# Two-expert routing after attention: the experts' up products as three fp32r products, with weight parts made for each tile

## The reference, cut to what matters

```python
x = L0_attn_x                                   # (2, 1024, 512) float32: 2048 tokens
xn = _layernorm(x)
x = x + attention(xn) + ffn(xn)

def ffn(x):                                     # 8 experts, two for each token, I = 352
    probs = softmax(einsum('th,eh->te', x, gate_w))
    topw, sel = top_k(probs, 2)
    topw = topw / sum(topw)
    combine = zeros((T, E)).at[arange(T)[:, None], sel].add(topw)
    g, u = split(einsum('th,eoh->eto', x, w1))  # w1: (8, 704, 512), the up products
    act = silu(g) * u
    expert_out = einsum('eti,ehi->eth', act, w2)
    return einsum('eth,te->th', expert_out, combine)
```

## Time and profile before

| | |
|---|---|
| median of 3 executions | 932.34 us (927.40 to 936.08) |
| the profiled execution: time, span | 932.23 us, 930.4 us |
| busy: PE, PEld, DVE | 850.4, 524.0, 368.2 us |
| busy: ACT, POOL | 290.8, 272.6 us |
| granted TensorE clock, mean | 0.957 |
| `gu` matmuls of the tiles, L883 | x624, 197.4 us |
| `down` matmuls, L901 | x234, 107.0 us |

### The profile page before, as it was taken

The page is one execution under the profiler, slowest core; times in us unless marked ns, Lnnn a source line. Parts: engine busy times, 40 slices in busy tenths (PEclk is TensorE's granted clock), DMA queues, the critical chain, the costliest instruction groups (busy, mean ns, idle before and its releaser), DMA issues. The chain is left out here.

```text
span 930.4 us, 12421 instructions
## 1 busy us (share of the span) xinstructions
PE 850.4 (91%) x3661; PEld 524.0 (56%) x3662; DVE 368.2 (40%) x1137; ACT 290.8 (31%) x622; POOL 272.6 (29%) x352
## 2 busy tenths in 40 slices
PE   3889999389999999999999989999999999999990
PEld 3668988255555555555555434566666656666650
DVE  5983452574666666666674021111111111111110
ACT  3221221004545555556555400112221211222210
POOL 4781000305233242332331610033332323333330
PEclk9899999758999999999999998999999999999995
DMA  9386596876357666576730137536445455433326
GB/s 318 143 264 206 197 314 203 252 171 228 97 156 186 187 191 153 178 199 173 189 83 14 42 112 258 169 69 156 107 107 158 73 156 147 81 68 64 57 29 201
DMA packets 76716, 143.20 MB, mean 154 GB/s; under 512 B 12928, under 2 KB 26752, under 8 KB 76608
## 3 DMA queue, kind: packets, MB, share of 16 engines
q1 hardware_dynamic: 38192, 65.68, 22.7%
q10 hardware_dynamic: 29056, 58.28, 22.1%
q0 software_dynamic: 9424, 18.69, 10.8%
HBM read 81.21 MB, written 61.15 MB: 153 GB/s over the span
## 5 line engine op out<-in xcount | busy, mean ns | idle before, releaser
L1286 ACT ACTIVATE probs<-scores_t 128x512 f32<-128x512 f32 (+3 forms) x384 | 163.7, 492 | 143.8 <-PE scores_t L1413 130.2
L883 PE MATMUL gu<-w,rows_t 128*128 x624 | 197.4, 459 | 1.1 <-DVE o_t L849 1.1
L1390 PE MATMUL maxima<-k_stack,q_stack 96*128 96x512 f32 (+3 forms) x384 | 141.2, 388 | 14.7 <-DMA q_stack<-qk_hi 8.7
L883 PEld LDWEIGHTS gu<-w,rows_t 128*128 128x128 f32 x624 | 115.2, 190 | 69.7 <-issue 19.7
L1433 PE MATMUL o_acc<-probs,v_ones 128*64 128x512 f32 (+3 forms) x768 | 147.9, 507 | 0.0
L1413 PE MATMUL scores_t<-q_stack,k_stack 98*128 98x512 f32 (+3 forms) x384 | 138.0, 385 | 5.6 <-DMA q_stack<-row_lo 3.5
L1316 DVE CUSTOM_DVE_ANT_0 masked_scores<-maxima,mask_m 128x128 f32<-128x128 f32 (+3 forms) x256 | 121.3, 485 | 23.5 <-PE maxima L1390 19.3
L1320 DVE TENSOR_REDUCE mx<-maxima 128x1 f32<-128x512 f32 x128 | 88.2, 689 | 86.4 <-PE maxima L1390 86.3
L1413 PEld LDWEIGHTS scores_t<-q_stack,k_stack 98*128 98x128 f32 x384 | 73.1, 193 | 67.9 <-issue 42.2
L901 PE MATMUL down<-w,hidden_t 128*128 (+1 forms) x234 | 107.0, 592 | 0.8 <-DVE hidden_t L857 0.8
L1390 PEld LDWEIGHTS maxima<-k_stack,q_stack 96*128 96x128 f32 x384 | 76.8, 202 | 35.6 <-DVE mx L1320 9.9
(11 more groups left out here) (148 smaller groups left out, 930.7 us busy)
## 6 DMA issues: line engine op xcount, KB each, us to landing
w<-in_w_t SPq DMA_DIRECT2D x8, 1408.0 KB, 6.5
routed<-blank_row ACTq DMA_DIRECT2D x20, 514.0 KB, 6.9
rows<-routed ACTq DMA_DIRECT2D x39, 256.0 KB
qk_hi<-st_hi SPq DMA_DIRECT2D x32, 256.0 KB, 4.8
qk_lo<-st_lo SPq DMA_DIRECT2D x32, 256.0 KB, 6.1
q_stack<-qk_hi ACTq DMA_DIRECT2D x32, 256.0 KB, 4.1
k_stack<-qk_hi ACTq DMA_DIRECT2D x26, 256.0 KB, 5.2
v_all<-o_t SPq DMA_DIRECT2D x4, 1536.0 KB, 5.7
```

What stands on the lines that cost most here:

```text
L883: last = nc.tensor.matmul(gu[r][j][:, 0:I], rows_t[r][:, k * P:(k + 1) * P], w1[:, bass.ds(e, 1), k, j * I:(j + 1) * I].rearrange("p o n - ...
L1286: nc.scalar.activation(probs[:, k % PR, h, 0:w], scores_t[e % RING][:, 0:w], ACT.Exp).then_inc(exp_done, 1)
L1390: nc.tensor.matmul(mb[at % RING][:, 0:w], q_st[i][0:3 * HD, h, t * P:(t + 1) * P], k_st[i][0:3 * HD, h, c * CH:c * CH + w], start=True, st ...
```

## The change

The up products become three fp32r products each (24 matmuls for a tile in place of 8 fp32 ones, which the trace shows as 16 records). The rows are split in PSUM-to-SBUF copies: ScalarE makes `rows_hi`, VectorE `rows_lo`. The high and low parts of the expert's `w1` (128 x 4 x 704) are made anew for every tile, one tile ahead: four ScalarE copies and four VectorE subtractions, two of each ahead of the old work of the tile and two behind it. ScalarE and VectorE read the ring slot from memory into a register; PE tells ScalarE by `tile_ready` that the expert of the next tile has been loaded. Each expert gets at least one tile, by one more small VectorE operation in the router (the tile counts with these inputs stay as the router finds them, and the loops always run over 39).

```diff
+        link(V.tensor_scalar(tiles[:], tiles[:], 1.0, None, ALU.max))
...
-        rows_t = [m.sbuf(f"rows_t{r}", [P, D], F32) for r in range(2)]
+        rows_hi = [m.sbuf(f"rows_hi{r}", [P, D], F32R) for r in range(2)]
+        rows_lo = [m.sbuf(f"rows_lo{r}", [P, D], F32R) for r in range(2)]
+        w1_hi = [m.sbuf(f"w1_hi{r}", [P, DK, 2 * I], F32R) for r in range(2)]
+        w1_lo = [m.sbuf(f"w1_lo{r}", [P, DK, 2 * I], F32R) for r in range(2)]
...
@@ sync: weights
                 load_weights(e)
-            for e in range(RING_E):
-                announce(e)
+                if e:
+                    announce(e - 1)
+            announce(RING_E - 1)
@@ scalar
-                nc.scalar.copy(rows_t[r][:], turn_ps[:]).then_inc(turned_read, 1)
+                nc.scalar.copy(rows_hi[r][:], turn_ps[:]).then_inc(rows_hi_done, 1)
+            def up_weights_high(r, slot, ks):
+                for k in ks:
+                    nc.scalar.copy(w1_hi[r][:, k, :], w1_rows(slot, k)).then_inc(w1_hi_done, 1)
+            def await_up_weights(i):
+                if past(i, 2):
+                    act.wait_ge(gu_full, (i - 1) * 2)
+                act.wait_ge(tile_ready, i + 1)
+                return slot_at(act, i)
             def tile(i, r, half):
                 if past(i, 2):
                     y_to_sbuf(i - 2, r, half - 1)
+                if more:
+                    slot = await_up_weights(i + 1)
+                    up_weights_high(1 - r, slot, range(0, DK // 2))
                 act.wait_ge(gu_full, i * 2 + 1)
                 ...
                 nc.scalar.activation(gated[:], gu[r][0][:, 0:I], ACT.Silu).then_inc(silu_done, 1)
+                if more:
                     rows_to_sbuf(i + 1, 1 - r)
+                    up_weights_high(1 - r, slot, range(DK // 2, DK))
                 load_rows(i + 3, 1 - r)
             for a in range(LATE):
                 if a == LATE - 1:
+                    up_weights_high(0, await_up_weights(0), range(DK))
                     rows_to_sbuf(0, 0)
@@ vector
+            def rows_low(i, r):
+                dve.wait_ge(rows_hi_done, i + 1)
+                ...
+                nc.vector.tensor_tensor(rows_lo[r][:], turn_ps[:], as_f32(rows_hi[r][:]), ALU.subtract).then_inc(turned_read, 1)
+            def up_weights_low(i, r, slot, ks):
+                if past(i, 2):
+                    dve.wait_ge(gu_full, (i - 1) * 2)
+                for k in ks:
+                    dve.wait_ge(w1_hi_done, i * DK + (k + 1))
+                    nc.vector.tensor_tensor(w1_lo[r][:, k, :], w1_rows(slot, k), as_f32(w1_hi[r][:, k, :]), ALU.subtract).then_inc(w1_done, 1)
             def tile(i, r, half):
+                if more:
+                    slot = slot_at(dve, i + 1)
+                    up_weights_low(i + 1, 1 - r, slot, range(0, DK // 2))
                 hidden_to_sbuf(i - 1, 1 - r)
+                if more:
+                    rows_low(i + 1, 1 - r)
+                    up_weights_low(i + 1, 1 - r, slot, range(DK // 2, DK))
                 ...
                 nc.vector.tensor_tensor(hidden[r][:], gu[r][1][:, 0:I], gated[:], ALU.mult).then_inc(hidden_done, 1)
             for a in range(LATE):
                 ...                                   # the adds into o_t, L849
+                if a == LATE - 2:
+                    up_weights_low(0, 0, slot_at(dve, 0), range(DK))
+            rows_low(0, 0)
@@ tensor
+                    nc.tensor.matmul(out, hi, w1_hi[r][:, k, cols], start=(k == 0), stop=False)
+                    nc.tensor.matmul(out, hi, w1_lo[r][:, k, cols], start=False, stop=False)
+                    last = nc.tensor.matmul(out, lo, w1_hi[r][:, k, cols], start=False, stop=(k == DK - 1))
             def tile(i, r, half):
                 if past(i, 2):
+                    down_product(i - 2, r, slot_at(pe, i - 2))
+                announce_tile(i + 1)
                 pe.wait_ge(turned_read, i + 1)
                 ...
-                pe.wait_ge(expert_ready, e + 1)
+                pe.wait_ge(w1_done, i * DK + DK)
+            def announce_tile(i):
+                pe.wait_ge(expert_ready, expert_at(pe, i) + 1)
+                pe.sem_inc(tile_ready, 1)
```

More of the change, by code:

```diff
@@ L727, in run_tiles, with expert_at, slot_at, w1_rows @@
                 tile(i, i % 2, i // 2)
+        def expert_at(engine, i):
+            return engine.value_load(tile_expert[0:1, bass.ds(i, 1)], min_val=0, max_val=E - 1)
+        def slot_at(engine, i):
+            return engine.value_load(keep["tile_slot"][0:1, bass.ds(i, 1)], min_val=0, max_val=RING_E - 1)
+        def w1_rows(slot, k):
+            return w1[:, bass.ds(slot, 1), k, :].rearrange("p o n -> p (o n)")
         def past(i, least):
@@ L817, in tile @@
                     y_to_sbuf(i - 2, r, half - 1)
+                more = not (isinstance(i, int) and i == SLOT_TILES - 1)
+                if more:
+                    slot = await_up_weights(i + 1)
+                    up_weights_high(1 - r, slot, range(0, DK // 2))
                 act.wait_ge(gu_full, i * 2 + 1)
@@ L844, in _ @@
         def _(dve):
[L845 to L850, removed]
             def hidden_to_sbuf(i, r):
@@ L866, in tile @@
                 nc.vector.tensor_tensor(hidden[r][:], gu[r][1][:, 0:I], gated[:], ALU.mult).then_inc(hidden_done, 1)
+            for a in range(LATE):
+                at = EARLY + a
+                dve.wait_ge(proj_full, a + 1)
+                nc.vector.tensor_tensor(o_t[:, :, at * P:(at + 1) * P], gu[a % 2][a // 2 % 2][:].rearrange("p (g t) -> p g t", t=P),
+                                        res[:, at, :].rearrange("p (g t) -> p g t", t=P), ALU.add).then_inc(res_done, 1)
+                if a == LATE - 2:
+                    up_weights_low(0, 0, slot_at(dve, 0), range(DK))
+            rows_low(0, 0)
             run_tiles(dve, tile)
@@ L879, in turn_rows, with up @@
                 last.then_inc(turned, 1)
-            def up(i, r, e, j):
+            def up(i, r, j):
+                out = gu[r][j][:, 0:I]
                 for k in range(DK):
-                    last = nc.tensor.matmul(gu[r][j][:, 0:I], rows_t[r][:, k * P:(k + 1) * P],
-                                            w1[:, bass.ds(e, 1), k, j * I:(j + 1) * I].rearrange("p o n -> p (o n)"),
-                                            start=(k == 0), stop=(k == DK - 1))
+                    hi, lo = (t[r][:, k * P:(k + 1) * P] for t in (rows_hi, rows_lo))
+                    cols = slice(j * I, (j + 1) * I)
+                    nc.tensor.matmul(out, hi, w1_hi[r][:, k, cols], start=(k == 0), stop=False)
+                    nc.tensor.matmul(out, hi, w1_lo[r][:, k, cols], start=False, stop=False)
+                    last = nc.tensor.matmul(out, lo, w1_hi[r][:, k, cols], start=False, stop=(k == DK - 1))
                 last.then_inc(gu_full, 1)
@@ L904, in down_product @@
                 last.then_inc(y_full, 1)
[L906 to L910, removed]
             def tile(i, r, half):
                 if past(i, 2):
[L914 to L917, removed]
+                    down_product(i - 2, r, slot_at(pe, i - 2))
+                if not (isinstance(i, int) and i == SLOT_TILES - 1):
+                    announce_tile(i + 1)
                 pe.wait_ge(turned_read, i + 1)
@@ L935, in _ @@
                     pe.wait_ge(res_done, a - 3)
+                if a == LATE - 2:
+                    announce_tile(0)
                 if a == LATE - 1:
```

14 lines of the change are left out of this document (9 added, 5 removed).

## The result

The changed kernel takes 939.55 us (median of 20 executions, 934.18 to 945.84) against 932.34 for the kernel before: ratio 1.008, 95% interval 1.0057 to 1.0103. It is 0.8% slower: clear of the scatter between executions, and inside the 1% that the prediction called no change. (One of the 20 executions of the kernel before took 1116.68 us; it stands alone and isn't compared.) The profiled execution took 937.0 us, its span 935.1.

The account below looks back on a forecast made before the run. PE's instructions were taken to bound each tile, all else hidden. Saving 33.5 us, plus 4.6 start, 16 late tags and 11.5 clock, gives -1.4 from 932.2, so 930.8; forecast 930 us, range 908 to 955.

Parts of the forecast that it names:

- the sign: Whole kernel: slightly faster, the sum of terms being -1.4 us against the kernel before.
- the turning point: Tiles, under the port conflict rival: a ring over 7.5 us decides the sign, 37 tiles then giving back 10 us.
- What PE saves: Up products on PE: 0.86 us saved a tile, 8.08 to 7.22 us; 33.5 us over 39 tiles.
- What ACT and DVE get: Weight and row splits: ACT comes to 4.5 and DVE to 5.0 of 7.22 us a tile, covered as sums.
- The room: Chain from y to hidden_t before the down product: 0.55 us to spare, so PE still sets an undisturbed tile.
- The late tags: At the loads of experts 3 to 7, late y delays the down product 3.2 us, five times: +16 us.
- The clock: PE's clock falls to half speed behind the stalls: 2.3 us each, 11.5 for five (from 0 to 15.5).
- The start: Ahead of and in the first tiles, parts of tile 0 delay PE: +4.6 us (1 to 8).
- The ring from y over the scatter and the tag load to the next y: In the tiles, from one y to the next: 6.90 us, under the 7.22 us tile by little.
- the rival without room: Chain through ACT and DVE takes 7.4 to 7.6 us a tile: 37 x 0.3 = +11, 941 us; chance 0.16.
- The port conflict: Rival: GpSimd's scatter and VectorE's low parts delay each other; ring 7.6 to 8.3 us, 957 at 7.9; chance 0.17.

Follow-up runs that it names:

- the kernel before with the tag first: Kernel before, with GpSimd loading the tag of tile i+1 ahead of its wait for y of tile i: 932.5 us, ratio 0.9993.
- without reloads: Changed kernel without the loads of experts 3 to 7, whose tiles use the weights of experts 0 to 2: 914.59 us, ratio 0.9814.
- y behind: Changed kernel with y of tile i-2 taken on ScalarE behind the first two high parts of tile i+1, not ahead: 914.74 us, ratio 0.9805.
- the tag first: Changed kernel with GpSimd loading the tag of tile i+1 ahead of its wait for y of tile i: 919.64 us, ratio 0.9847.
- without rows: Changed kernel without the loads of rows for tiles 3 to 38, which use the rows in the buffers: 926.34 us, ratio 0.9924.
- parts once: Changed kernel with weight parts made for tiles 0 and 1 only and used by all later tiles: 913.03 us, ratio 0.9775.
- all three: Changed kernel with the tag's load first, y behind the high parts and tile 0's parts made early: 913.55 us, ratio 0.9779.
- the early parts: Changed kernel with tile 0's weight parts made two groups of the output projection earlier: 936.26 us, ratio 1.0037; other kernels add this edit to further ones.

## Why the prediction was right and wrong

The value, 930, is 9.6 us too low, inside its range; the sign, slightly faster, was wrong. The sum stood only 1.4 us under the kernel before, so any missing term of that size turned it; the prediction put the turning point at a ring over 7.5 us, but by its own 37 tiles 1.4 us are reached at 7.26. By its steps:

- *What PE saves, 0.86 us a tile: right.* Products begin 0.16 us apart, and the tile with nothing late is 7.22 us (mean of 7.17 and 7.27). Tiles before come 8.08 apart where no tag is late (7.99 and 8.17 in turn in the kernel before with the tag first). Only the number of tiles was a little high: 30.7 us between first and 39th y and, by the same 0.86, 1.7 for the two tiles' up products ahead of the first y, 32.4 in place of 33.5.
- *What ACT and DVE get: right.* Low parts 0.88 us each, 1.69 for a pair; y starts at T, high part at T+0.86 (forecast T+0.6), low at T+1.78, `hidden_t` done at T+4.0 (T+3.69), down product at T+4.14 (T+3.84). The room was 0.3 us less, 0.25 and not 0.55.
- *The late tags: right in mechanism, place, number and size.* Five stalls behind five weight loads, released by `hidden_t`; forecast 3.2 us each and 16 in all, measured 3.17 to 3.60 and 16.8. They go in the kernel without reloads, shrink to 1.3 to 1.7 us with y behind, and the kernel before has none.
- *The clock: right in kind, half in size.* It fell behind three of five stalls and cost 5.6 us; forecast were 11.5 for five. One cost 1.9 us, near the 2.3 forecast; two of the five cost nothing.
- *The start: too small.* The section is 4.4 us longer, but it holds 1.7 of PE's saving, so the start costs 6.1 where +4.6 was forecast: PE's first up product comes 3.0 later by the marks in place of 1.7 (idle 4.04 us in place of 2.8; the first high part began 2.4 us after the add and not 1.3), the next wait is 1.29 for 1.4, and the half-speed stretch cost some 1.7 for 1.5.
- *The step that failed is "The ring from y over the scatter and the tag load to the next y ... 6.90 us ... That is under 7.22, by little."* 6.90 is the ring with a tag landing after 4.1 us: the row was taken while y was catching up, when the load of rows had gone out 2 us earlier. The median landing stood in the earlier trace rows, 4.7, and with it the ring is 2.65 + 4.7 + 0.2 = 7.55, over 7.22. The turn of 7.2 and 7.8 gives back 6.5 us in the changed kernel and 8 to 9 in the one without reloads, where the sum has nothing. The prediction had priced this size under the rival without room (+11, 941), but put it down to the chain through ACT and DVE; the runs with the tag first and without rows show that it is the ring, together with the 0.25 us of room that such a y overruns.
- *The port conflict didn't happen in the changed kernel.* The scatter takes 1639 ns as before it did 1.64, the low parts 875 to 896 ns whether it runs beside them or not. The rule of the Trainium skill (SBUF — State Buffer, SBUF: two separate sides) gives no slowdown in these rows. But the runs have the conflict elsewhere. GpSimd's small `carrier` operation has two SBUF inputs and in the changed kernel never runs beside low parts. With the tag first it does, and takes 655 ns in the mean and up to 1.75 us, low parts unchanged at 884; in the kernel before with the same edit, without low parts, it takes 194 (that kernel's row is the second):

```profile
L803 POOL TENSOR_TENSOR carrier_y<-ident 128x1 f32<-128x1 f32 x39 | 25.5, 655 | 22.0 <-ACT y L839 18.6 <-DMA acc<-y,tag 3.0
...
L787 POOL TENSOR_TENSOR carrier_y<-ident 128x1 f32<-128x1 f32 x39 | 7.6, 194 | 48.4 <-ACT y L813 45.0 <-DMA acc<-y,tag 3.1
```

  So that rival priced the wrong instruction: the scatter of the changed kernel isn't held up, an operation on GpSimd with both inputs in SBUF is, which is the case that the rule names. What kept the first stage's subtractions 1.27 us apart in the earlier trace rows was not tried.

By sections of the profile the sum is -32.4 (PE) + 6.1 (start) + 16.8 (stalls) + 1.5 (the rest of the late intervals) + 5.6 (clock) + 6.5 (turn) - 0.6 (end) = +3.5 us, and the measured sections give +3.4. The two profiles differ by 4.7 us, the medians by 7.2. Of the rest, 1.3 us lie ahead of the first add, where both kernels run almost the same code and the profiles scatter. The other 2.5 lie between the changed kernel's profiled execution (937.0 us, granted clock 0.949) and its median; over its 20 executions the slower ones have the lower clock (0.950 at 934.18 us, 0.935 at 945.84). Behind which idle times it fell in them no trace shows.

That 930 isn't further off is partly luck: the clock was forecast 5.9 us too dear, the ring 6.5 too cheap.

## What to carry to other kernels

Sums of busy time said that ACT and DVE had room, and they had; what cost the gain was one waiting instruction at the head of a queue whose followers PE needs soon. Before new work is put on a covered engine, look for the instruction ahead of it that waits for a DMA, and put the new work in front of it, or take the DMA out of the loop: a load of 1 KB was worth 36 us here (939.55 against 903.61) once PE had 0.86 us less a tile. And when a ring is compared with a tile, take its time from rows with the median landing, not from where it is catching up: those are among its fastest.

## What the runs showed of the hardware that wasn't expected

- **An idle time's length alone doesn't say whether the clock falls.** Behind 3.17 and 3.33 us of idle time the down product ran at full speed (2.84 us), behind 3.28 at 4.54 and 3.43 at 5.48; in the kernel without loads of rows, 2.51 us left it at full speed and 2.56 didn't (timeline of PE of that kernel):

```profile
681.48 4.54 PE L957 MATMUL down<-w,hidden_t 128*128 x6 [2.56 <-DVE hidden_t L880]
...
796.58 2.84 PE L957 MATMUL down<-w,hidden_t 128*128 x6 [2.51 <-DVE hidden_t L880]
```

  Nor is there a safe length among the short ones. None of the waits of 1.7 us or less in the tiles was followed by the lower clock, nor were 2.04 us (parts once) and 2.69 (all three); but 1.81 to 1.90 us in tile 1 were, in all four kernels with the early parts.
- **A 1 KB load sees its neighbours.** Issued when the last scatter has landed, the tag lands after 1.9 us in the median. Issued 1.06 us behind a scatter, it takes 4.1 with no loads of 256 KB in the tiles, 4.9 to 5.3 with one issued 0.2 to 0.3 us behind it, and 7.9 to 8.6 behind the 2.1 MB of an expert. An indirect add of rows is held up there too (9.3 us to landing at most, 5.4 in the median).
- **VectorE holds GpSimd up, but not in every instruction.** Low parts (two SBUF inputs) beside a scatter: no change in either (884 and 1639 ns). Beside a two-input operation of 128x1 on GpSimd: the low parts stay at 884, the small operation takes 655 ns in the mean in place of 194.
